# Sixteen experts summed in PSUM instead of on VectorE: gates spread over the partitions by a selector product, multiplied into the transposed input, and the residual taken through the shared matrix

## The reference

```
s      = softmax(u @ centroids.T + expert_biases)          # 16 experts
g      = s where s is one of the two largest, else 0        # a token's gates
xe     = einsum('bsd,eod->bseo', u, Wr) + br                # every expert's output
routed = einsum('bse,bseo->bso', g, xe)
shared = (einsum('bsd,eod->bso', u, Ws) + sum(bs)) / 2      # two shared experts
return u + routed + shared
```

## Time and profile before

| what | value |
|---|---|
| time, median of 3 runs | 1455.34 us (1453.94 to 1456.78) |
| the profiled execution | 1455.86 us, of which the span is 1454.0 us |
| busy share of PE, DVE, ACT, POOL | 91%, 70%, 50%, 40% |
| granted TensorE clock, mean over the span | 0.941 of full |
| MOE stage | about 323 to 581 us of the span |

### The profile page before, as it was taken

The page is one execution under the profiler, slowest core; times in us unless marked ns, Lnnn a source line. Parts: engine busy times, 40 slices in busy tenths (PEclk is TensorE's granted clock), DMA queues, the critical chain, the costliest instruction groups (busy, mean ns, idle before and its releaser), DMA issues.

```text
span 1454.0 us, 30116 instructions
## 1 busy us (share of the span) xinstructions
PE 1316.1 (91%) x9370; PEld 983.1 (68%) x9370; DVE 1024.2 (70%) x2849; ACT 730.8 (50%) x2292; POOL 584.9 (40%) x761
## 2 busy tenths in 40 slices
PE   4999999977888786699999999999999986799997
PEld 2777777753444443577777777777777764699997
DVE  5455555547887788676777777777778764688886
ACT  2232333312223222387777777777777875444442
POOL 3221211123555456555555555565555542111111
PEclk9999999978778778799999999999999997899999
DMA  8000000000000000000000000000000000000000
GB/s 254 1 1 1 0 0 0 0 1 1 1 0 0 0 0 0 1 2 2 2 1 2 2 0 0 0 0 0 0 0 0 1 1 1 1 9 14 11 11 16
DMA packets 14271, 12.23 MB, mean 8 GB/s; under 512 B 1764, under 2 KB 12536, under 8 KB 13944
## 3 DMA queue, kind: packets, MB, share of 16 engines
q1 hardware_dynamic: 14200, 11.33, 2.5%
HBM read 9.23 MB, written 2.10 MB: 8 GB/s over the span
## 4 chain that ended last, share of the span: by engine, by line
PE 58%; DVE 14%; ACT 12%; issue 9%; POOL 4%; DVEq 0%; ACTq 0%; POOLq 0%
PE bank L167 11%; PE bank L757 10%; PE bank L1019 8%; PE bank L528 7%; PE bank L477 6%; PE bank L1032 5%; ACT work L976 4%; PE bank L939 3%; ACT work L998 3%; ACT work L956 2%; ACT work L1026 1%; DVE work L1187 1%; DVE work L1179 1%; ACT work L928 1%; POOL rstd L342 1%
## 5 line engine op out<-in xcount | busy, mean ns | idle before, releaser
L956 ACT ACTIVATE work<-bank,work 128x256 f32<-128x256 f32 x512 | 235.5, 504 | 32.0 <-DVE work L948 31.9
L948 DVE TENSOR_REDUCE work<-bank 128x2 f32<-128x512 f32 x256 | 159.0, 684 | 125.0 <-PE bank L939 125.0
L970 POOL TENSOR_TENSOR work<-work 128x512 f32<-128x512 f32 x128 | 130.6, 1041 | 251.2 <-DVE work L964 251.2
L757 PE MATMUL bank<-WrT,xT 128*128 128x512 f32 x256 | 163.4, 786 | 34.2 <-DVE moe_work L777 33.7
L340 POOL TENSOR_SCALAR ve<-mv 128x2 f32<-128x2 f32 x128 | 29.4, 229 | 408.9 <-DVE mv L278 408.9
L922 POOL TENSOR_TENSOR work<-work 128x512 f32<-128x512 f32 x128 | 160.6, 1276 | 29.1 <-DVE work L912 29.1
L486 DVE TENSOR_TENSOR la_work<-bank,tri 128x512 f32<-128x512 f32 x128 | 87.8, 686 | 84.6 <-PE bank L477 84.5
L1019 PE MATMUL bank<-work 128*64 128x256 f32 x1024 | 129.3, 394 | 16.4 <-DVE work L1005 16.4
L990 PE MATMUL bank<-ident,work 128*128 128x128 f32 x1024 | 139.4, 280 | 1.7 <-ACT work L998 0.9
L939 PE MATMUL bank<-work 32*128 32x256 f32 x2048 | 130.4, 391 | 6.5 <-POOL work L922 3.6
L990 PEld LDWEIGHTS bank<-ident,work 128*128 128x128 f32 x1024 | 113.5, 142 | 30.7 <-issue 26.0
(11 more groups left out here) (166 smaller groups left out, 2879.4 us busy)
## 6 DMA issues: line engine op xcount, KB each, us to landing
X<-in_x SPq DMA_DIRECT2D x4, 512.0 KB, 5.8
wF<-in_L_ffn_h_w SPq DMA_DIRECT2D x2, 1024.0 KB, 9.3
out<-X SPq DMA_DIRECT2D x16, 128.0 KB, 1.8
w_qkv<-in_L_attn_w_qkv SPq DMA_DIRECT2D x1, 1536.0 KB, 9.7
WrT<-in_L_ffn_Wr SPq DMA_DIRECT2D x1, 1024.0 KB
w_out<-in_L_attn_w_out SPq DMA_DIRECT2D x1, 512.0 KB, 11.3
wF<-in_L_ffn_w_w SPq DMA_DIRECT2D x2, 256.0 KB, 10.2
rope_sin<-in_rope_sin SPq DMA_DIRECT2D x1, 256.0 KB
```

Source lines behind the costliest of these rows:

```text
L757: ins = nc.tensor.matmul(unit_bank(p, b, t)[:, :], xT[:, p, t * P:(t + 1) * P], WrT[:, b * BLK:(b + 1) * BLK], start=True, stop=True)
L948: nc.vector.tensor_reduce(nmax[:, QUAD * a + j, :], SB_[j][:, :].rearrange("p (t k) -> p t k", t=T), AX.X, ALU.max, negate=True).then_inc( ...
L956: ins = nc.scalar.activation(pr[:, a % 2, j, t, :], SB_[j][:, t * LEN:(t + 1) * LEN], ACT.Exp, bias=nmax[:, h, t:t + 1], accum_out=psum_[: ...
L970: nc.gpsimd.tensor_tensor(pr[:, a % 2, j, :, :], pr[:, a % 2, j, :, :], parts, ALU.mult).then_inc(c_pn, 1)
```

## The change

It turns the MOE product around. The gates go through TensorE: `gT` now has 128 partitions, with the gates rounded to fp32r in partitions 0 to 15, what the rounding lost in 32 to 47 (`moe_low_vector`, new, VectorE), and 0.5 in 64 and 65 for the shared experts' biases. A product with a selector matrix `sel` (`moe_spread_tensor`, new) copies one expert's gates to all 128 partitions, token by token along the columns; two experts (a pair) fill one PSUM bank of 128x512. An elementwise product of that bank with the transposed input `XnT` gives the gated input `xg`. VectorE does this for six pairs of the eight (`moe_scaled_vector`); for pairs 3 and 7 ScalarE copies the bank to SBUF and GpSimd multiplies (`moe_far_scalar`, `moe_far_pool`). `moe_pair_tensor` multiplies the gated input (stationary) by the experts' weights (moving) and adds all experts up in one PSUM bank. The residual comes through the shared matrix: `Wsh` is now half the sum of the shared weights plus the identity. The norm of round 2 reads its statistics and its input from PSUM. The additions L777, L788, L795, L799, L804 and L766, and the copy L356, are gone. GpSimd's order in a step is changed too, and it builds `sel`, the split biases and the constant part of the gates once, in step 2 of the LA stage.

```diff
+        sel = first_set.enter_context(nc.sbuf_tensor("sel", [P, EXPERTS, P], F32R))
+        gT = first_set.enter_context(nc.sbuf_tensor("gT", [P, 2, LEN], F32R))
+        br_hi = first_set.enter_context(nc.sbuf_tensor("br_hi", [P, E], F32R))
+        br_lo = first_set.enter_context(nc.sbuf_tensor("br_lo", [P, E], F32R))
...
+
+        def pairs_done(i, k):
+
+            return DVE_PAIRS * i + 3 * (k // 4) + k % 4 + 1
+
+        def far_done(i, k):
+
+            return 2 * i + k // 4 + 1
...
-            nc.scalar.activation(gT[:, p, :], RB[0:EXPERTS, 256:256 + LEN], ACT.Copy).then_inc(b_gs, 1)
+            nc.scalar.activation(gT[:, p, :], RB[:, 256:256 + LEN], ACT.Copy).then_inc(b_gs, 1)
...
+        def moe_low_vector(dve, i, p):
+
+            dve.wait_ge(b_gs, i + 1)
+            nc.vector.tensor_tensor(gT[32:64, p, :], RB[32:64, 256:256 + LEN], gT[32:64, p, :], ALU.subtract)\
+                .then_inc(b_lo, 1)
+
+        def moe_spread_tensor(pe, i, p, k):
+
+            if k == 0:
+                pe.wait_ge(b_lo, i + 1)
+            if k % 4 == FAR:
+                pe.wait_ge(b_ge, reached(far_done(i, k) - 1))
+            else:
+                pe.wait_ge(b_xg, reached(pairs_done(i, k) - 3))
+            for e in range(2):
+                ins = nc.tensor.matmul(XB[k % 4][:, e * LEN:(e + 1) * LEN], sel[:, 2 * k + e, :], gT[:, p, :],
+                                       start=True, stop=True)
+            ins.then_inc(b_gk, 1)
+
+        def moe_scaled_vector(dve, i, k):
+
+            dve.wait_ge(b_main, reached(XPAIRS * i + k - 3))
+            wait_apart(dve, b_gk, XPAIRS * i + k + 1, s_x[0], 16)
+            x2 = seq_cols(XnT, i).rearrange("p (o l) -> p o l", o=1).to_broadcast([P, 2, LEN])
+            nc.vector.tensor_tensor(xg[:, k % 4, :].rearrange("p (o l) -> p o l", o=2),
+                                    XB[k % 4][:, :].rearrange("p (o l) -> p o l", o=2), x2, ALU.mult)\
+                .then_inc(b_xg, 1)
+
+        def moe_far_scalar(act, i, k):
+            act.wait_ge(b_gk, XPAIRS * i + k + 1)
+            act.wait_ge(b_xgp, reached(far_done(i, k) - 1))
+            nc.scalar.activation(gs, XB[k % 4][:, :], ACT.Copy).then_inc(b_ge, 1)
+
+        def moe_far_pool(pool, i, k):
+            pool.wait_ge(b_main, reached(XPAIRS * i + k - 3))
+            wait_apart(pool, b_ge, far_done(i, k), s_nhalf, 1)
+            x2 = seq_cols(XnT, i).rearrange("p (o l) -> p o l", o=1).to_broadcast([P, 2, LEN])
+            nc.gpsimd.tensor_tensor(xg[:, k % 4, :].rearrange("p (o l) -> p o l", o=2),
+                                    gs.rearrange("p (o l) -> p o l", o=2), x2, ALU.mult).then_inc(b_xgp, 1)
...
             for t in range(T):
-                o = SHB[:, t * E:(t + 1) * E]
-                nc.tensor.matmul(o, xT[:, p, t * P:(t + 1) * P], Wsh[:, :], start=True, stop=False)
-                nc.tensor.matmul(o, gT[:, p, t * P:(t + 1) * P], br[:, :], start=False, stop=False)
-                ins = nc.tensor.matmul(o, half[:, :], bs[:, :], start=False, stop=True)
+                tokens = slice(t * P, (t + 1) * P)
+                nc.tensor.matmul(moe_y(p)[:, t, :], xT[:, p, tokens], Wsh[:, :], start=(t == 0), stop=False)
+                nc.tensor.matmul(moe_y(p)[:, t, :], gT[:, p, tokens], br_lo[:, :], start=False, stop=False)
+                ins = nc.tensor.matmul(moe_y(p)[:, t, :], gT[:, p, tokens], br_hi[:, :], start=False, stop=False)
...
+        def moe_pair_tensor(pe, i, p, k):
+
+            if k % 4 == FAR:
+                pe.wait_ge(b_xgp, far_done(i, k))
...
+                pe.wait_ge(b_xg, pairs_done(i, k))
+            for e in range(2):
+                for t in range(T):
+                    x_ = xg[:, k % 4, e * LEN + t * P:e * LEN + (t + 1) * P]
+                    ins = nc.tensor.matmul(moe_y(p)[:, t, :], x_, WrT[:, (2 * k + e) * E:(2 * k + e + 1) * E],
+                                           start=False, stop=(k == XPAIRS - 1 and e == 1 and t == T - 1))
+            ins.then_inc(b_main, 1)
...
+        MOE_ORDER = (("norm", 0), ("norm", 1), ("pair", 4), ("router", 0), ("pair", 5), ("router", 1), ("norm", 2),
+                     ("pair", 6), ("router", 2), ("router", 3), ("norm", 3), ("norm", 4), ("router", 4), ("router", 5),
+                     ("router", 6), ("router", 7), ("norm", 5), ("norm", 6), ("norm", 7), ("low", 0), ("next", 0),
+                     ("norm", 8), ("next", 1), ("next", 2))
...
+                if i_is(i, 2):
+                    nc.gpsimd.memset(gp.rearrange("p a t e -> p (a t e)"), 0.0).then_inc(s_gp, 1)
+                    pool.wait_ge(s_gp, 1)
+                    nc.gpsimd.memset(gp[:, :, :, 64:66], 0.5).then_inc(s_gp, 1)
+                    pool.wait_ge(s_const, 16 * 8)
+                    nc.gpsimd.tensor_copy(sel[:, :, :], own[:, :].rearrange("p (e o) -> p e o", o=1)
+                                          .to_broadcast([P, EXPERTS, P])).then_inc(s_sel, 1)
+                    pool.wait_ge(s_br, 16 * 3)
+                    nc.gpsimd.tensor_copy(br_hi[:, :], br[:, :]).then_inc(s_brhi, 1)
+                    pool.wait_ge(s_brhi, 1)
+                    nc.gpsimd.tensor_tensor(br_lo[:, :], br[:, :], br_hi[:, :], ALU.subtract).then_inc(s_brlo, 1)
...
             def moe_step(i, p):
                 lag = not i_is(i, 0)
                 if lag:
                     rstd_pool(pool, 2, i - 1, 0)
-                    residual_pool(pool, 2, i - 1)
-                    rstd_pool(pool, 2, i - 1, 1)
-                moe_block_pool(pool, i)
-                ffn_excess_pool(pool, i, p)
                 if not i_is(i, SEQS - 2, SEQS - 1):
                     pool_xT(pool, MOE, i + 2, p)
                 if lag:
+                    residual_pool(pool, 2, i - 1)
+                moe_far_pool(pool, i, 4 + FAR)
+                if lag:
+                    rstd_pool(pool, 2, i - 1, 1)
                     rstd_pool(pool, 2, i - 1, 2)
+                if not i_is(i, SEQS - 1):
+                    moe_far_pool(pool, i + 1, FAR)
+                ffn_excess_pool(pool, i, p)
```

238 lines of the change are left out of this document (98 added, 140 removed).

## The result

| | before | after |
|---|---|---|
| median of the timed runs | 1455.47 us (1453.94 to 1456.78) | 1471.18 us (1468.92 to 1474.92) |
| ratio, 95% interval | | 1.0110, 1.0096 to 1.0124 |
| profiled execution: time, span | 1455.86 us, 1454.0 us | 1470.92 us, 1469.1 us |
| mean granted clock | 0.941 | 0.941 |

A forecast was written before the change was run, and what follows sets the result against it. It took a loop of waits through the third root to bound the MOE step (15.9 us). New steps of 17.2 us end the stage 8.8 us later; less 1.5 given back, +7.3 on 1455.86 gives 1462.7 us, range 1440 to 1484.

The forecast's parts named there:

- What bounds the kernel before: MOE stage: a loop of waits through GpSimd's third inverse root sets the step, 15.9 us.
- The chain: New MOE step: ten links over four engines, from one sequence's low gates to the next's, 15.6 us at full clock.
- link 1: Chain's start on TensorE: spreads 0 to 3 with product 7 between, 2.1 us at full clock.
- well under 1.3 us: Sign of a wrong prediction: GpSimd's product for pair 3 or 7 taking well under the 1.3 us assumed.
- links 7 and 10: Chain: negated maximum and ScalarE's exponentials, 1.3 us; VectorE's `xa`, statistics and low gates, 1.8 us.
- links 8 and 9: Chain: ScalarE copies pair 7, 0.8 us; GpSimd multiplies it, 1.3, then root 1, 1.1; the gates hidden beside them.
- The clock: MOE step: TensorE's waits put link 1 at half clock in 17 of 20 steps, +1.6 us, to 17.2 us.
- the clock stays full: Faster rival: TensorE keeps full clock in MOE, step 15.6 us, total 1438.4 us; chance 0.30 with its partial forms.
- about 9: VectorE's busy time in an MOE step falls from 12.7 us to about 9, so it is no bound.
- a longer chain: Slower rival: slow `xa` beside GpSimd and costlier hand-overs, step 18.3 us, total 1478 us; chance 0.14.
- The MOE stage's length: First gates at 335.8, then 14 x 17.2 us and 13.5 for the last sequence: end at 590.1, 8.8 later.
- Given back: MOE to SA seam: SA's first products follow busy TensorE work instead of a standstill, saving 1.5 us.

The follow-up runs named there:

- e4_filler: The changed kernel with two unneeded TensorE products a step ahead of the transposes of the gates; ratio to the kernel before 1.0032.
- e5_p6_early: The changed kernel with product 6 ahead of the gates' transposes and product 7 ahead of spreads 0 and 1 on TensorE; ratio to the kernel before 0.9979.
- e7_combo: The changed kernel with the edits of e2_sa_both, e3_test_early and e5_p6_early together; 1415.96 us, ratio to the kernel before 0.9725.
- e9_combo_order: e7_combo with VectorE's second norm application and negated maximum moved ahead of pairs 5 and 6; 1399.05 us, ratio to the kernel before 0.9606.
- e12_order_all_dve: e9_combo_order with the edits of e6_all_dve, pair 7 standing behind pair 6 on VectorE; ratio to the kernel before 0.9677.
- e6_all_dve: The changed kernel with pairs 3 and 7 multiplied by VectorE from PSUM, without ScalarE's copies and GpSimd's products; ratio to the kernel before 0.9893.
- e3_test_early: The changed kernel with GpSimd's weights test ahead of the multiplication of the next sequence's pair 3; ratio to the kernel before 0.9931.
- e1_sa_input: The changed kernel with GpSimd's splits of SA's first inputs moved into the last two MOE steps; ratio to the kernel before 1.0069.
- e2_sa_both: e1_sa_input with TensorE's transposes of sequence 14's normalization 2 moved behind SA's first four units; ratio to the kernel before 1.0055.

## Why the prediction was right or wrong

- **What bounds the kernel before: wrong.** That the loop passes through the third root is not so (two runs, ratios 1.0003 and 0.9990): it is TensorE's work at the clock that it gets, with one wait of 2.2 us for VectorE, and the 15.9 us are the mean of steps of 14.6, 16.4 and 16.9. It cost the forecast nothing, since the step was taken from the trace as measured.
- **The chain: right in its order, and nearly so in each link.** From the rows above, measured against forecast: link 1 from the low gates' end to the copy 3.9 us (3.7 with the half clock), copy 0.8 (0.8), pair 3 1.05 (1.3), test 2.7 (2.7), root 0 1.1 (1.1), `yn` and pair 6 1.2 (1.3), negated maximum and exponentials 1.4 (1.3), copy 0.7 (0.8), pair 7 and root 1 2.1 (2.4), `xa`, statistics and low gates 1.9 (1.8). GpSimd's product takes 1.09 us from SBUF here, less than the 1.30 of the earlier trace rows; "well under 1.3 us" was one of the forecast's signs of being wrong, and its 0.4 us a step were made up in part by 0.2 us more in link 1 and 0.1 each in links 7 and 10. A hand-over from ScalarE to GpSimd, put at 0.1 without a row, takes 0.14 to 0.25. The gates were to be hidden beside links 8 and 9 with 1.7 us to spare; 0.16 was left.
- **The clock: right in its price, not in its waits.** 1.6 us a step, seen at both levels in one execution of e4_filler (15.4 and 17.05 us). The two waits of 1.8 and 2.2 us were one of 3.4 us, ahead of the transposes. Behind the 3.4 us of the changed kernel the half clock came in every step. For shorter waits there is no such rule in these runs: e4_filler and e5_p6_early have steps at 1.00 and at 0.80 to 0.90 behind the same waits of 1.4 to 1.7 us. The rival "the clock stays full" came true in e7_combo, e9_combo_order and e12_order_all_dve, with waits of 1.2 to 2.5 us a step in all.
- **VectorE at "about 9" us of a step: too low**, it is 11.7 (152.67 of 221.8 us, 13 steps). The 24 additions gave back 7.1 us and not 8.2, since their records overlap (112.9 us busy in 16 sequences); a product out of PSUM costs 0.69, not 0.60, for nothing overlaps it here; and of the four comparisons (L710) of a step one takes 1.06 to 1.22 us beside GpSimd's product where the others take 0.28 (in e6_all_dve, without that product, all take 0.29). It was no bound, so nothing came of it here, but it put the second chain, which e3_test_early found, closer than I thought.
- **The rival "a longer chain": its ground did not hold.** `xa` took 344 ns in the mean, the 334 of the chain and not the 772 of the kernel before.
- **The MOE stage's length: 2.9 us too long.** The gates of sequence 1 came at 335.7 (forecast 335.8), which is luck in part: the stage began 1.2 us earlier than in the trace that the forecast started from, and the 1.8 us for the half clock had been taken with 0.11 us for a pass, not the 0.118 of the line before. Those of sequence 15 came at 572.0 (576.6): 13 steps at 17.06 and the first at 14.5. The last sequence took 15.2 us instead of 13.5. Product 7 ended at 587.2, forecast 590.1.
- **The failed step: "Given back".** I let SA's first product start where product 7 ends, and took off 1.5 us for a clock that would be full. The measured term is a gap of +6.6 us, 8.1 us from the forecast. The other 2.6 us behind it (1.6 in SA's first step and 1.0 in the rest) are within what executions of the same code differ by, and the 2.9 us by which the stage was too long in the forecast hid part of the miss. I asked what TensorE does next, but not what else the next product waits for: the split behind the last test (2.6 us, e1_sa_input) and the transposes behind a normalization of two more rounds (the rest, e2_sa_both). The old stage had hidden both under VectorE's additions. Without the gap, as in e2_sa_both, the change costs 8.0 us, and the 1.5 us still do not come back.
- **`sel` and the split biases for nothing: right.** TensorE's busy time and clock in the LA stage are unchanged, and the stage ends no later than before; a shift under 2 us could not be told from the spread of the runs.
- **The rule on engine selection** (the Trainium skill, GPSIMD Engine Reference, section 4.1 Engine selection) was said to make the chain about 3 us shorter. e6_all_dve had the step 2.3 us shorter (part of it by a clock of 0.93 instead of 0.80) and the kernel 32 us faster, so the trace agrees. In e12_order_all_dve, with the other waits shortened, the same edit cost 10 us, so it is no rule for every order.

## What to carry to other kernels

When a stage gets shorter work on its main engine, ask of the next stage's first instruction everything that it waits for, in every queue: preparations that the old stage covered come out at the seam. A wait that is booked on an engine is not yet on the loop: move its cause in the old kernel and see, before building on it, and look at single steps, since a mean of 15.9 us can hide steps of 14.6 and 16.9. And TensorE's clock is a term of its own: two useless products a step made this kernel 11 us faster, and with the waits shortened the whole stage had 1.00. A microsecond or two behind the changed stage is to be held against other executions of the same code before a cause is given to it.
